# A graph kernel's preparation rewritten: counts by products of four groups, inverses kept by node, and the input's normalisation in the same stage

## The reference, cut to what matters

```
h   = relu(layernorm(x))
x   = x + gcn4(h, src, dst)          # weights 1/sqrt(degree of both ends)
h   = relu(layernorm(x))
for i in 0..2:                       # relational layers
    seg = dst * 16 + type
    agg = segment_sum(h[src], seg)               # N x 16 x 128
    cnt = segment_sum(ones, seg)                 # N x 16
    agg = agg / max(cnt, 1)
    h   = einsum('nrd,rdo->no', agg, W[i]) + h @ root[i] + bias[i]   (relu but for the last)
x = x + h
```

## Time and profile before

| | us |
|---|---|
| median of three runs (lowest, highest) | 3733.86 (3727.67, 3737.41) |
| the profiled execution's own time | 3700.42 |
| its span | 3698.7 |
| mean granted TensorE clock in it | 0.921 |

### The profile page before, as it was taken

The page is one execution under the profiler, slowest core; times in us unless marked ns, Lnnn a source line. Parts: engine busy times, 40 slices in busy tenths (PEclk is TensorE's granted clock), DMA queues, the critical chain, the costliest instruction groups (busy, mean ns, idle before and its releaser), DMA issues.

```text
span 3698.7 us, 82678 instructions
## 1 busy us (share of the span) xinstructions
PE 2784.9 (75%) x25480; PEld 1786.5 (48%) x25481; DVE 2202.9 (60%) x7982; ACT 1375.2 (37%) x3073; POOL 1211.2 (33%) x1250
## 2 busy tenths in 40 slices
PE   3211666667689999958888888788888878888887
PEld 1110333333355565535555556555555555555555
DVE  6666888888664534325555555455555555555555
ACT  0322777777632222023333332333333333333332
POOL 1002000000000000015555554455555545555554
PEclk9555888888899999979999999899999989999999
DMA  0002000001111101154444444444444444444443
GB/s 23 0 8 58 37 35 35 35 35 37 58 43 30 56 17 49 56 154 124 121 122 123 127 122 114 118 122 128 121 122 122 121 119 122 124 124 125 122 122 85
DMA packets 197029, 315.97 MB, mean 85 GB/s; under 512 B 36705, under 2 KB 131276, under 8 KB 196924
## 3 DMA queue, kind: packets, MB, share of 16 engines
q1 hardware_dynamic: 155932, 226.92, 20.8%
q0 software_dynamic: 40992, 87.70, 8.4%
HBM read 269.54 MB, written 44.95 MB: 85 GB/s over the span
## 4 chain that ended last, share of the span: by engine, by line
PE 23%; issue 12%; DMA 11%; DVE 4%; another core or an unknown queue 3%; POOL 2%; DVEq 1%; ACT 1%; POOLq 0%; SPq 0%; ACTq 0%
DMA arena<-pair,arena 11%; PE psum L1939 8%; PE psum L1952 6%; PE psum L1963 4%; PE psum L1916 3%; POOL arena L1856 2%; DVE arena L2128 2%; PE psum L1929 1%; DVE arena L2124 1%; DVE arena L2134 1%; DVE arena L2164 1%; PE psum L1890 1%; DVEq L2157 0%; DVEq L2164 0%
## 5 line engine op out<-in xcount | busy, mean ns | idle before, releaser
L1856 POOL DMA_INDIRECT arena<-pair,arena x1212 | 1159.3, 956 | 910.3 <-issue 335.2
L2134 DVE SCALAR_TENSOR_TENSOR arena<-psum,arena,work 128x304 f32<-128x304 f32 x606 | 313.2, 518 | 766.7 <-DMA h<-h 564.0
L1952 PE MATMUL psum<-arena 128*128 128x304 f16 x3939 | 580.0, 294 | 49.2 <-issue 46.4
L2067 ACT ACTIVATE arena<-psum 128x1024 f16<-128x1024 f32 x303 | 310.2, 1024 | 780.8 <-DMA h<-h 311.8
L1939 PE MATMUL psum<-arena 128*128 128x304 f16 x2424 | 380.4, 297 | 182.6 <-DMA arena<-pair,arena 159.2
L1092 PE MATMUL psum<-arena,h 128*128 128x512 f16 x1750 | 481.8, 381 | 19.9 <-DMA h<-h 19.9
L2128 DVE TENSOR_SCALAR arena<-arena 128x304 f16<-128x304 f16 x2121 | 487.1, 300 | 0.0
L1952 PEld LDWEIGHTS psum<-arena 128*128 128x128 f16 x3939 | 360.6, 98 | 242.1 <-issue 129.6
L1963 PE MATMUL psum<-arena 128*128 128x152 f32 (+1 forms) x2496 | 383.6, 299 | 25.7 <-DVE arena L2134 24.5
L1093 PE MATMUL psum<-arena,h 128*128 128x128 f16 x1750 | 384.7, 220 | 0.0
L1916 PE MATMUL psum<-arena 128*32 128x256 f16 x7272 | 328.5, 279 | 63.6 <-issue 57.6
(11 more groups left out here) (258 smaller groups left out, 3430.2 us busy)
## 6 DMA issues: line engine op xcount, KB each, us to landing
work<-winv SPq DMA_DIRECT2D x303, 304.0 KB
arena<-pull SPq DMA_DIRECT2D x303, 224.0 KB
pull<-rows SPq DMA_DIRECT2D x101, 224.0 KB
arena<-pair,arena POOLq DMA_INDIRECT x1212
h<-work SPq DMA_DIRECT2D x12, 640.0 KB, 3.3
h<-h POOLq DMA_DIRECT2D x12, 640.0 KB, 7.5
pair<-arena SPq DMA_DIRECT2D x12, 256.0 KB
x_pad<-arena SPq DMA_DIRECT2D x1, 1600.0 KB, 7.3
```

Source lines behind the costliest of these rows:

```text
L1856: e.indirect_dma_start(out=t.msg[:, j, k].rearrange("p h f -> p (h f)"), out_offset=None, in_=d[f"pair_{l}"].rearrange("n h f -> n (h f)") ...
L1952: m = e.matmul(p.psum[:, 1, 0:KEYS], t.smsg[:, j % 2, tile, half, :], t.soh[:, j % 2, tile, :], start=(tile == 0 and half == 0), stop=(til ...
L2067: e.activation(t.smsg[:, q, 0:4].rearrange("p k h f -> p (k h f)"), p.psum[:, GATHER:GATHER + 2, :].rearrange("p b n -> p (b n)"), ACT.Cop ...
L2134: e.scalar_tensor_tensor(t.agg[h % 2][:, :, k % BATCH, :], p.psum[:, k % 2, 0:KEYS].rearrange("p (r w) -> p r w", r=REL), t.back[:, l:l + ...
```

## The change

Four things are done.

1. **Counts.** Edge types and places in the window are cast to 16 bits and laid out so that the tiles of four neighbouring groups lie on four separate rows. DVE makes all one-hots with 35 comparisons against a constant over 100 columns of each of four groups, then 35 over the remaining 104 (16 types and 19 places; ACT fills rows 16 to 31 of each quarter with something finite that is not read). PE multiplies a 128x128 operand (four groups times 32) by a 128x76 one (four groups times 19), 4 products to a round, 51 rounds; each 16x19 table on the diagonal lies on its own 32 partitions. DVE adds it into `quarters` (128 partitions by 3200 nodes); an add waits for the one four before it. x is loaded in this stage.
2. **Inverses by node.** PE multiplies each 128-node block of `quarters` by a 128x17 selection, which gives nodes on partitions, 16 counts and the degree. The inverse is taken on 128 partitions by 400, and stored as `inverse[node, type]`. `relations` loads it per group, from a base node read into a register: two transfers per pair, 19 nodes by 16 types. The mean reads it with types in the inner place.
3. **One stage.** The inverses and the input's normalisation are one stage; both roots are taken at once; ACT makes the upper halves, DVE the lower, by groups of five blocks; the stores of halves, keys and inverses are waited for in the next stage (`saved`), by POOL, ahead of the zeroing there.
4. **Zeroing moved.** POOL zeroes `quarters` and 7 blocks in `slots` (from when PE's counts there are done), 11 blocks in the joined stage; 3 by POOL and 4 by DVE are left for `build_adjacency`.

```diff
...
+        for a, z in PARTS:                                   # columns 0:100, 100:204 of each group row
+            for r in range(REL):
+                e.tensor_scalar(t.hot_r[:, :, r, a:z], typ[:, :, a:z], float(r), None, ALU.is_equal)
+            for w in range(RWIN):
+                one = e.tensor_scalar(t.hot_c[:, :, w, a:z], dloc[:, :, a:z], float(w), None, ALU.is_equal)
+            one.then_inc(s_hot, 1)
+        for n in range(NG):
+            if n % LOAD == 0 and n + LOAD < NG:
+                e.load(regs[n // LOAD % 2 ^ 1][0:more], t.gbase[0:1, n + LOAD:n + LOAD + more])
+            to = t.quarters[32 * q:32 * q + REL, bass.ds(base, RWIN)]
+            if q == 0:
+                e.wait_ge(s_mm, min(ROUNDS, (m // PER_BANK + 1) * PER_BANK))
+            if n >= G:
+                e.wait_ge(s_ad, n - G + 1)
+            e.tensor_tensor(to, to, p.psum[32 * q:32 * q + REL, bank, at + q * RWIN:at + (q + 1) * RWIN],
+                            ALU.add).then_inc(s_ad, 1)
...
+            for k in range(GT):
+                x = e.matmul(p.psum[0:n * 32, bank, at:at + n * RWIN],
+                             t.hot_r[:, 0:n, :, m * GT + k].rearrange("p g r -> p (g r)"),
+                             t.hot_c[:, 0:n, :, m * GT + k].rearrange("p g w -> p (g w)"),
+                             start=(k == 0), stop=(k == GT - 1))
...
+def inverses_and_norm(p, t, n):
...
+    @block.sync
+    def _(e):
+        e.dma_start(d["x_pad"].rearrange("(b p) f -> p b f", p=P), t.x).then_inc(s_x, 16)
+        e.wait_ge(s_key, 1)
+        e.dma_start(d["key_pt"][:, :], t.wgt).then_inc(p.saved, 16)
+        e.wait_ge(s_inv, 2)
+        e.dma_start(d["inverse"].rearrange("(b p) r -> p b r", p=P), n.inverse).then_inc(p.saved, 16)
+        for q in range(GROUPS):
+            e.wait_ge(s_lo, q + 1)
+            e.dma_start(d["h16_0"][q * GN:q * GN + GN].rearrange("(b p) h f -> p b (h f)", p=P),
+                        n.h0[:, q * GB:q * GB + GB].rearrange("p b h f -> p b (h f)")).then_inc(p.saved, 16)
+        e.wait_ge(s_x, 16)
+    @block.gpsimd
+    def _(e):
+        e.wait_ge(s_key, 1)
+        for b in (0, 1) + tuple(range(NORM_TO, EARLY_FROM)):
+            zero_adjacency(e, p, b, b + 1).then_inc(s_z, 1)
...
+    @block.vector
...
+        e.scalar_tensor_tensor(t.wgt, t.typf, float(RWIN), t.dloc, ALU.mult, ALU.add).then_inc(s_key, 1)
+        moments(v, e, t.x, n.stats, n.mv, BLOCKS, p.sem("passed"))
+        v.inc(e.tensor_scalar(n.value[:, BLOCKS:], n.mv[:, :, 1], EPS, None, ALU.add))
+        e.wait_ge(s_dg, 1)
+        v.link(e, e.tensor_scalar(n.value[:, 0:BLOCKS], counts[:, :, REL], 1.0, None, ALU.add))
+        e.sem_inc(s_sq)
+        e.tensor_scalar(n.inverse, counts[:, :, 0:REL], 1.0, None, ALU.max).then_inc(s_inv, 1)
+        e.wait_ge(s_inv, 1)
+        e.reciprocal(n.inverse, n.inverse).then_inc(s_inv, 1)
+        e.wait_ge(s_sq, 2)
+        inverse_root(v, e, n.root, n.value, n.tmp)
...
+        for b in range(BLOCKS):
+            e.tensor_scalar(t.x[:, b, :], t.x[:, b, :], n.mv[:, b, 0:1], n.root[:, BLOCKS + b:BLOCKS + b + 1],
+                            ALU.subtract, ALU.mult).then_inc(s_y, 1)
+        for q in range(GROUPS):
+            a, z = q * GB, (q + 1) * GB
+            e.wait_ge(s_y, z)
+            e.wait_ge(s_hi, q + 1)
+            e.scalar_tensor_tensor(n.h0[:, a:z, 1, :], t.x[:, a:z, :], 0.0, n.h0[:, a:z, 0, :], ALU.max,
+                                   ALU.subtract).then_inc(s_lo, 1)
...
+    @block.tensor
+    def _(e):
+        e.wait_ge(s_sel, 2)
+        for b in range(BLOCKS):
+            m = e.matmul(counts[:, b, :], t.quarters[:, b * P:(b + 1) * P], n.choice, start=True, stop=True)
+        m.then_inc(s_dg, 1)
...
+        e.wait_ge(p.saved, p.saves)
+        e.sem_inc(s_go)
-        zero_adjacency(e, p, ZEROED, ZEROED + 3).then_inc(s_z, 1)
+        zero_adjacency(e, p, 2, 5).then_inc(s_z, 1)
-        zero_adjacency(e, p, ZEROED + 3, BLOCKS).then_inc(s_z, 1)
+        e.wait_ge(s_go, 1)
+        zero_adjacency(e, p, 5, NORM_TO).then_inc(s_z, 1)
...
+        e.wait_ge(s_ct, 1)
+        e.memset(t.quarters, 0.0).then_inc(s_clear, 1)
+        for b in range(EARLY_FROM, BLOCKS):
+            zero_adjacency(e, p, b, b + 1).then_inc(s_clear, 1)
...
-            e.dma_start(t.winv[j // HALF][:, at:at + 2, :], d["winv"][rows].rearrange("g r w -> g (r w)")
-                        .partition_broadcast(P)).then_inc(s_wi[j], 16)
+            for g in range(2):
+                base = e.snap(bases[2 * j + g], min_val=0, max_val=NODES - 1)
+                e.dma_start(t.winv[j // HALF][:, at + g, :], d["inverse"][bass.ds(base, RWIN), :].rearrange("n r -> (n r)")
+                            .partition_broadcast(P)).then_inc(s_wi[j], 16)
         weights(0)
+        e.wait_ge(s_ky, 32)
+        windows_of(slice(0, TURN), TURN)
...
-                                   t.winv[h % 2][:, k % BATCH, :].rearrange("p (r w) -> p r w", r=REL),
+                                   t.winv[h % 2][:, k % BATCH, :].rearrange("p (w r) -> p r w", r=REL),
```

More of the change, by code:

```diff
@@ L438, in count_relations @@
 def count_relations(p, t):
[L442 to L446, removed]
-    block = Bodies()
+    d = p.d
+    G = 4
+    NG = EDGE_TILES // GT
+    ROUNDS = -(-NG // G)
+    HALF_AT = 25
+    PER_BANK = 6
+    WIDE = G * RWIN
+    LOAD = 12
+    PARTS = (0, HALF_AT * GT), (HALF_AT * GT, ROUNDS * GT)
+    whole = (BLOCKS - 1) * P
+    s_16, s_hot, s_rest, s_mm, s_ad, s_tail, s_x = (p.sem(n) for n in (
+        "halves", "hot", "rest", "counted", "added", "tail", "x"))
@@ L449, in _ @@
+    @block.gpsimd
+    def _(e):
+        e.memset(t.x[:, BLOCKS - 1, :], 0.0).then_inc(s_tail, 1)
     @block.vector
     def _(e):
[L451 to L480, removed]
+        regs = [[e.alloc_register(f"cnt_base{q}_{k}") for k in range(LOAD)] for q in range(2)]
+        e.tensor_copy(spread(t.typ16), edges(t.typf)).then_inc(s_16, 1)
+        e.tensor_copy(spread(t.dloc16), edges(t.dloc)).then_inc(s_16, 1)
+        typ, dloc = (a.rearrange("p (g n) -> p g n", g=G) for a in (t.typ16, t.dloc16))
@@ L482, in _ @@
     @block.scalar
     def _(e):
[L484 to L492, removed]
@@ L493, in _ @@
-        copy(ROUNDS - 1, 0)
+        e.wait_ge(s_16, 1)
+        typ = t.typ16.rearrange("p (g o n) -> p g o n", g=G, o=1)
+        for a, z in PARTS:
+            for g in range(G):
+                e.activation(t.hot_r[:, g, REL:, a:z], typ[:, g, :, a:z].to_broadcast([P, 32 - REL, z - a]),
+                             ACT.Copy).then_inc(s_rest, 1)
     @block.tensor
     def _(e):
[L497 to L560, removed]
@@ new lines, in _ @@
+        e.wait_ge(s_hot, 1)
+        e.wait_ge(s_rest, G)
+        for m in range(ROUNDS):
+            n = min(G, NG - m * G)
+            bank, at = place(m)
+            if m == HALF_AT:
+                e.wait_ge(s_hot, 2)
+                e.wait_ge(s_rest, 2 * G)
+            if m >= 8 * PER_BANK:
+                e.wait_ge(s_ad, PER_BANK * G)
+            for k in range(GT):
[3 more added lines that the diff above has]
+                             start=(k == 0), stop=(k == GT - 1))
+            x.then_inc(s_mm, 1)
@@ L597, in first_norm @@
     block = Bodies()
[L599 to L604, removed]
     @block.sync
@@ L652, in norm_memory @@
     return t
+def norm_memory(p, t):
+    n = Bag()
+    c = p.carve(t.free)
+    n.h0 = c(BLOCKS * RF, F16).rearrange("p (b h f) -> p b h f", b=BLOCKS, h=2)
+    n.stats = c(BLOCKS * 6).rearrange("p (b s) -> p b s", b=BLOCKS)
+    n.mv = c(BLOCKS * 2).rearrange("p (b s) -> p b s", b=BLOCKS)
+    n.value, n.root, n.tmp = c(2 * BLOCKS), c(2 * BLOCKS), c(2 * BLOCKS)
+    n.choice = c(REL + 1)
+    n.inverse = c(BLOCKS * REL).rearrange("p (b r) -> p b r", b=BLOCKS)
+    assert p.at <= NORM_TO * NPAD // 2, p.at
+    return n
 AT = 8
```

124 lines of the change are left out of this document (94 added, 30 removed).

## The result

Median 3641.2 us (3639.5 to 3643.8, four runs) against 3732.3 us for the kernel before (3727.7 to 3737.4, four runs). The ratio is 0.9757, 95% interval 0.9742 to 0.9773: the kernel is faster by 91 us, inside the wide range, but not in the likeliest case's own range (3585 to 3635). The forecast was 126 us.

A forecast was written before the change was run, and what follows sets the result against it. Rewritten stages were each priced by their critical engine, the count stage by DVE's chain of adds, `relations` mostly by PE. Terms +7 - 56 - 78 - 1 + 2 = -126 from 3734 gave 3608 us; wide range 3580 to 3665.

The forecast's parts named there:

- the likeliest case: The whole kernel at 3608 us, all terms as summed, own range 3585 to 3635; chance 0.62.
- Slots: In `slots`, POOL's added zeroing holds DVE's string of short instructions: 7 us lost, between 0 and 12.1.
- the 12.1 us bound: In `slots`, DVE held at every chance loses the whole time of POOL's zeroing, up to 12.1 us.
- Count stage: Stage counting edges, ending on DVE with PE hidden: 67 us against 122.9, so -56 (-68 to -28).
- rival 1: Count stage: PE's operands with a 408-byte step slow the products, stage ends on PE: +33, so 3641 us; chance 0.12.
- the adds and their loads: Count stage on DVE: 202 adds at 0.18 us, 36 us (28 to 61); 16 register loads at 0.61, 10 us (5 to 14).
- Rival 4: Count stage: adds stay at 0.30 us, paced by the wait on the fourth before or register arithmetic: +25, 3633 us; chance 0.10.
- Inverses and norm: Joined stage of inverses and input normalisation: 32 us against 110.1, so -78 (-82 to -72).
- Preamble: Start of the adjacency stage: wait for the last store, less zeroing by DVE: -1 us (-3 to +2).
- Relations: The layers' stage: two inverse transfers per pair hidden, same bytes, only the start waits longer: +2 us (0 to +50).
- The strided mean: `relations`: the mean's 64-byte-step read costs nothing, at most 0.32 us on 518 ns; DVE has 304 us free per layer.
- Rivals 2 and 3: `relations`, strided mean: partly on the path, +23 to +45, about 3642 (chance 0.12); wholly, +194, 3802 (chance 0.04).

The follow-up runs named there:

- e4: Changed kernel with POOL's early zeroing in `slots` begun one signal later, after DVE's short string: 0.9744 of the kernel before; count stage begins at 95.27 us, not 100.94.
- e8: Changed kernel with the 202 adds at fixed addresses, no register loads or register arithmetic (wrong counts): count stage 57.0 us instead of 77.9; only that stage is read.
- e5: Changed kernel with one transfer of inverses per pair, from the first group's base (second group's inverses wrong): 0.9685 of the kernel before, a pair 6.62 us.
- e6: Changed kernel, still two transfers per pair, addresses from the loop's counter, no register loads on SP (wrong inverses): 0.9749 of the kernel before, a pair 6.71 us.
- e7: e4 plus windows copied to a table by group inside the adjacency stage, one transfer per pair in relations: 0.9685 of the kernel before, median 3609.0 us.
- e3: Kernel before, each pair's inverses loaded in two transfers of 1216 bytes a partition instead of one of 2432: ratio 1.0038, 14 us slower, a pair 6.56 us.
- e1: Changed kernel, the mean reading inverses in one run, without the 64-byte step (wrong pairing): 0.9744 of the kernel before; the mean 533 ns from 723.
- e2: Kernel before, the mean reading its inverses with a step of 64 bytes (wrong pairing): ratio 0.9998, the mean 729 ns, a pair 6.52 us.
- e11: e7 with two transfers of 1216 bytes per pair from the table by group: 0.9821 of the kernel before in the 3339 us set, a pair 5.53 us.

## Why the prediction was right in sign and range, and 35 us off in size

- **Slots: right, 6.3 for 7.** The trace shows DVE held instruction by instruction, and e4 takes that away. The rule of the Trainium skill on the exclusive lock (SBUF — State Buffer, Who interferes with whom) agrees with the trace; the 12.1 us bound was not reached, because DVE's passes over PSUM and with two inputs went on beside the memsets.
- **Count stage: the mechanism right, a term mis-sized.** It ends on DVE, PE is hidden (0.14 us a product, under the 0.26 at which it would bind; rival 1 did not come, but no run reads these operands without the step of 408 bytes, so whether it is part of the 0.14 is open). Comparisons cost 12.3 us for 70, not 17.5. The terms for the adds and their loads failed: I took 36 + 10 = 46 us, they took 61.7: 0.23 us an add instead of 0.18, and some 0.98 us a load instead of 0.61. The row that I took for a load had eight registers to fill; this one has twelve, which is the likely reason but was not varied. That a load prefetched by a block would still stop the adds was in the sum. The adds and loads give +16, the comparisons -5: of the 11 us missing here. Rival 4's 0.30 us did not come; part of the cause that it named did, since e8 puts 0.03 us of each add down to register work.
- **Inverses and norm: right, 31.3 for 32.** DVE waited 3.0 us for PE's counts in the middle, as forecast; POOL's memsets held one pass (0.83 us for 0.21).
- **Preamble: right within 1.5 us.**
- **Relations: the step that failed is "Bytes are the same; ... so 1216 is no small piece: nothing."** It priced the load by its bytes and by the rate at which 512-byte pieces were stored when alone. In company, these two transfers per pair cost 27 us against e5's one (24 by e6 against e5 in one set, 21 by e7 without e4's part; some 10 us of uncertainty each), which is as much as was missing here. e3 shows 14 us (9 to 19) for two transfers in the kernel before, with windows side by side and no more engine time; the rest goes with windows that overlap, by the packets' times, though the split is argued across sets and not shown within one. How the transfers reach the pair's period stays open; PE's longer waits at the first product with a pull table point at the pulls.
- **The strided mean: the cost was inside the bound (0.19 of at most 0.32 us), and off the path** (e1, e2), for the reason given: DVE has slack in each pair. Rivals 2 and 3 did not come. That the measured 3641 us is the very time that rivals 1 and 2 gave (3641, 3642) is chance: neither mechanism was at work. The Trainium skill's rule on 16-byte lines (Advanced Engine Details and Errata, SBUF Cachelines) agrees with the trace: a penalty of 0.62 ns an element read (189 ns over 304), 1.39 written; it was the price that was real and the path that was not.

The two misses, 11 and 27 us, less 3 for the small terms that came out better than forecast (slots 0.7, inverses and norm 0.8, preamble 1.5), are the 35 us between the forecast and the measured gain.

## What to carry to other kernels

Price a transfer in a busy loop by how many there are and where they read, not by bytes: over 303 steps the same bytes in two broadcast loads per step cost 14 us where the two read side by side, and about 27 where they overlapped. With overlapping reads the queue's packets took a fifth more engine time. A one-time copy into the shape that the loop loads, under another stage, gave back 21 us or more. Before moving an idle engine's memset beside another engine's string of short passes, look at what kind these are; starting it a few microseconds later cost nothing later on and gave the stage back 5.7 us.

## What the runs showed of the hardware

- The kernel before took 3729 to 3732, 3703 and 3339 us in different sets of runs, with the same code. Up to `relations` the times agree within some 10 us (1475.2 us in e11 in the fastest set, 1478.6 in e7); the difference lies in the pairs (5.5 against 6.5 to 6.7 us). In the fastest set PE waits 19 us for the gathered rows (e11, 1650 to 3200 us), in e7's 150 us over the same stretch. What differs between the sets is not shown; the record gives the 3703 and the 3339 set the same chip number.
- The share that a change brings depends on that: two transfers and late zeroing make 0.982 of before in the fastest set (e11); the one-transfer version was not run there. Nor was a plain mean: PE's waits for DVE are larger there than those for the gathered rows (in e11, 33.0 + 16.9 + 9.0 us against 18.8), so that the strided read is off the path is shown for the slower sets only.
- A DVE instruction of 304 columns with two inputs took 534 ns plain, 723 with one input at a step of 64 bytes, 958 with its output at a step of 608.
